# Layer 0 of a graph network: a dense product with a scattered matrix of edge weights, in place of edge-by-edge sums

## The reference, cut to what matters

```python
x = _layernorm(x + _L0_gnn_ref(x, src, dst, edge_weight, weight, bias))
...
# layer 0, with edge_row = src and edge_col = dst
gathered = edge_weight[:, None] * x[edge_col]
neigh = jax.ops.segment_sum(gathered, edge_row, num_segments=N_NODES)
out = x @ w_self + neigh @ w_neigh + bias
```

## Time and profile before

| | us |
|---|---|
| median of 3 runs | 4293.28 |
| lowest and highest run | 4287.72, 4300.4 |
| span of the profiled execution | 5597.1 |
| edge loop of layer 0 in the profile (first to last L606) | 63.5 to 909 |
| rows of layer 1 out in the profile | 1505 |
| look-up of layer 1 in the profile | 1510 to 2010 |

### The profile page before, as it was taken

The page is one execution under the profiler, slowest core; times in us unless marked ns, Lnnn a source line. Parts: engine busy times, 40 slices in busy tenths (PEclk is TensorE's granted clock), DMA queues, the critical chain, the costliest instruction groups (busy, mean ns, idle before and its releaser), DMA issues. The chain is left out here.

```text
span 5597.1 us, 67496 instructions
## 1 busy us (share of the span) xinstructions
PE 3296.1 (59%) x16088; PEld 2121.1 (38%) x16089; DVE 2608.5 (47%) x6268; ACT 1784.1 (32%) x3811; POOL 2329.1 (42%) x2110
## 2 busy tenths in 40 slices
PE   5566663111459965446702655671745565999998
PEld 4444442100337742223701522340623333444454
DVE  7666772010249884447201744680654458021213
ACT  3444441000349953334200133460033346020212
POOL 5777887777230046662174065306046640000000
PEclk7887886555679977667755866895866676999999
DMA  8988885100245532232512500004622231313131
GB/s 223 182 181 177 151 138 127 51 22 0 78 121 149 148 97 86 84 88 91 184 33 63 145 22 21 12 14 131 189 61 86 86 112 60 104 61 104 60 106 40
DMA packets 413937, 543.83 MB, mean 97 GB/s; under 512 B 139432, under 2 KB 303361, under 8 KB 413363
## 3 DMA queue, kind: packets, MB, share of 16 engines
q1 hardware_dynamic: 250806, 305.92, 19.5%
q0 software_dynamic: 126368, 178.93, 15.5%
q10 hardware_dynamic: 36573, 56.91, 2.9%
HBM read 404.03 MB, written 141.04 MB: 97 GB/s over the span
## 5 line engine op out<-in xcount | busy, mean ns | idle before, releaser
L981 PE MATMUL ps<-shared_sb,onehot 128*128 128x264 f32 (+1 forms) x1600 | 597.6, 491 | 381.2 <-issue 238.1
L2053 DVE TENSOR_TENSOR accum<-accum,ps 128x264 f32 (+1 forms) x1248 | 530.8, 425 | 528.1 <-issue 341.8
L606 POOL DMA_INDIRECT t_neigh<-resid_sb,idx_b x416 | 655.9, 1577 | 217.8 <-issue 99.5
L1289 ACT ACTIVATE onehot<-iota,drel 128x128 f32<-128x128 f32 x1248 | 381.7, 388 | 1057.2 <-PE ps L904 697.3
L1040 PE MATMUL ps<-score_sb,shared_sb 128*128 128x512 f16 (+1 forms) x3150 | 641.7, 364 | 17.8 <-DVE shared_sb L2082 17.7
L651 POOL DMA_INDIRECT score_sb<-table,idx_a x192 | 200.1, 1042 | 920.4 <-issue 459.6
L981 PEld LDWEIGHTS ps<-shared_sb,onehot 128*128 128x128 f32 x1600 | 315.2, 229 | 664.5 <-issue 596.7
L771 PE MATMUL ps<-score_sb,onehot 128*128 x832 | 299.8, 523 | 330.7 <-DVE onehot L1737 323.0
L651 POOL DMA_INDIRECT shared_sb<-table,idx_a x384 | 363.0, 945 | 240.1 <-ACT idx_a L1272 129.5
L628 POOL DMA_INDIRECT t_adj<-counts,early_sb x391 | 410.0, 1049 | 122.0 <-issue 122.0
L638 POOL TENSOR_SCALAR onehot<-iota,carry_d 98x512 bf16<-98x512 f32 x28 | 43.6, 1562 | 976.8 <-PE ps L1057 814.0
(11 more groups left out here) (390 smaller groups left out, 6578.7 us busy)
## 6 DMA issues: line engine op xcount, KB each, us to landing
score_sb<-t_adj SPq DMA_DIRECT2D x105, 640.0 KB, 3.9
accum<-t_hot SPq DMA_DIRECT2D x208, 256.0 KB
accum<-t_drel SPq DMA_DIRECT2D x208, 128.0 KB
shared_sb<-t_key SPq DMA_DIRECT2D x104, 256.0 KB
t_hot<-shared_sb SPq DMA_DIRECT2D x104, 256.0 KB
t_adj<-accum ACTq DMA_DIRECT2D x70, 320.0 KB
shared_sb<-t_adj SPq DMA_DIRECT2D x35, 640.0 KB, 9.3
t_neigh<-accum ACTq DMA_DIRECT2D x4, 3328.0 KB
```

Of the source, the lines that this page charges most:

```text
L606: pool.indirect_dma_start(t_neigh[u], bass.IndirectOffsetOnAxis(ap=idx_b[:, q * L0H + u:q * L0H + u + 1], axis=0), msg[:, q * L0H + u, :], ...
L981: pe.matmul(ps[:, RING[(HU * h + u) % len(RING)], 0:w], onehot[:, h % 2 * HU + u, :], around[g][place(g, i, h)][:, u, 0:w], start=True, st ...
L1289: last = act.activation(onehot[:, h % 2 * HU + u, :], iota[:, 0:P], ACT.Abs, bias=drel[:, bass.ds(step + u, 1)], scale=-1.0)
L2053: dve.tensor_tensor(to, to, bank.unsqueeze(1), ALU.add).then_inc(step_acc, 1)
```

## The change

The neighbour sums become one dense product. For each edge, DVE sums the weights of all edges of its tile that have the same key; POOL writes the 391 x 128 sums to their cells of a DRAM matrix `t_w` of 26 x 128 rows by 3200 columns, in 4 bytes (42.6 MB, zeroed at the start by ACT). Rows are destinations, with the 98 rows of the last tile taking cells that a tile's run shares with the tile before. The product x^T times this matrix gives the neighbour sums already turned, and the turns and table sums go. The matrix is loaded in two parts of columns (2048 and 1152), 26 tiles each, three buffers per part. Each tile of the first part waits until all scatters have landed. Between the tiles of the second part PE makes 16 of the 25 products with the layer's weights. The edge loop shrinks to 98 quads of compares. Other moves: the copy of `t_lo` and the weights of layer 1 are issued right after SP's loop, the bias fold of layer 1 is done ahead.

```diff
@@ constants
-L0U, L0H = 16, 4
-L0N = L0U // L0H
-L0IT = S // L0U
-L0K = S // L0H
+L0H = 4
+QUADS = ET // L0H
+FIRST = 12
+WT = NT + 1
+WCOLS = [2048, NP - 2048]
+W_ZERO = 1280
@@ buffers
+        w_ring = [resid_sb[:, 0:3 * WCOLS[0]].rearrange("p (r n) -> p r n", r=3),
+                  score_sb[:, NT * GW:NT * GW + 3 * WCOLS[1]].rearrange("p (r n) -> p r n", r=3)]
+        w_banks = [[(4 * f + v, 0, v * 512, 512) for f in range(DC) for v in range(4)],
+                   [at for f in range(DC) for at in ((2 * f, 0, 0, 512), (2 * f + 1, 0, 512, 512), (4, f * P, 1024, P))]]
@@ order of the scatters, and the order of products
+        for quads in [range(8 * m, 8 * m + 8) for m in range(10)] + [range(80, 89), range(89, QUADS)]:
+            w_order += [L0H * q + b for b in range(L0H) for q in quads if L0H * q + b < EDGES_T]
+        product_order = [("l0", t) for t in range(20)] + [("l1", t) for t in range(GRP)] + [("l0", t) for t in range(20, NT)]
+        product_order += [("l1", t) for t in range(GRP, NT)]
+        UNDER = 16
@@ SP
-            with sp.Fori(0, L0IT) as i:
...
+            with sp.Fori(0, QUADS // 2) as i:
+                for h in range(2):
+                    sp.wait_ge(*count("counted", 2 * i + h + 1))
+                    sp.wait_ge(*count("key_used", 2 * i + h + 1))
+                    sp.sem_inc(done("sp_go"), 1)
+                    sp.dma_start(wide_key[:, h, :], on_each(t_key, i * 2 * L0H + h * L0H, L0H)).then_inc(key_in[h], 16)
+                    sp.dma_start(wide_w[:, h, :], on_each(a["ew2"], i * 2 * L0H + h * L0H, L0H)).then_inc(key_in[h], 16)
...
+            w_rows = t_w.rearrange("(r c) o -> r (c o)", c=NP)
+            for part in range(2):
+                first = 0 if part == 0 else WCOLS[0]
+                for t in range(WT):
+                    if part == 0 and t < NT:
+                        sp.wait_ge(*count("w_landed", QUADS))
+                    elif part == 0:
+                        sp.wait_ge(*count("w_landed", QUADS))
+                    if t >= 3:
+                        sp.wait_ge(*count("w_used", part * NT + t - 2))
+                    rows_t = P if t < NT else EQ
+                    put(w_ring[part][0:rows_t, t % 3, :], w_rows[t * P:t * P + rows_t, first:first + WCOLS[part]], w_in[3 * part + t % 3])
@@ POOL
-            def l0_scatter(k, q, first=False):
...
+            def weight_sums():
+
+                pool.wait_ge(*count("w_zero", 16 * (WT // 2)))
+                for n, j in enumerate(w_order):
+                    pool.wait_ge(*count("counted", j // L0H + 3))
+                    if n >= 2 * NACC:
+                        pool.wait_ge(*written(0, n - 2 * NACC))
+                    pool.indirect_dma_start(t_w, bass.IndirectOffsetOnAxis(ap=w_x[:, j:j + 1], axis=0), w_sum[:, j:j + 1],
+                                            None).then_inc((moved + gath)[n % (2 * NACC)], 16)
...
+            weight_sums()
@@ PE
+            def weighted_rows(part, between=lambda t: None):
+
+                for t in range(WT):
+                    pe.wait_ge(w_in[3 * part + t % 3], 16 * (t // 3 + 1))
...
+                    for n, (bank, col, first, w) in enumerate(w_banks[part]):
...
+                        lhs = hrows[:, t, f * P:(f + 1) * P] if t < NT else x_carry[:, f * P:(f + 1) * P]
+                        mm = pe.matmul(ps[:, bank, col:col + w], lhs, w_ring[part][0:rows_t, t % 3, first:first + w], start=(t == 0 and col == 0), stop=(t == NT and (part, n) != (1, 2)))
...
+                    between(t)
...
+            weighted_rows(0)
...
+                def layer0(t):
+                    own = slice(t * P, (t + 1) * P)
+                    product("l0", t, [(cols[:, c, own], weights[:, c, 0:D]) for c in range(DC)]
+                            + [(neigh_w[:, c, own], weights[:, DC + c, 0:D]) for c in range(DC)])
...
+                weighted_rows(1, under)
+                for t in range(UNDER, 20):
+                    layer0(t)
+                layer1(0)
+                for t in range(20, NT):
+                    layer0(t)
+                for g in range(1, NG):
+                    layer1(g)
@@ ACT
+            no_sums = flat_a[:, 5376:5376 + W_ZERO].unsqueeze(1).to_broadcast([P, 2 * NP // W_ZERO, W_ZERO])
+            for part in t_w.rearrange("(k p n w) o -> k p n (w o)", k=WT // 2, p=P, w=W_ZERO):
+                act.dma_start(part, no_sums).then_inc(done("w_zero"), 16)
@@ DVE, one quad of the loop
+            def compare(i, h):
+                k = 2 * i + h
+                dve.wait_ge(key_in[h], 32 * i + 32)
                 dve.wait_ge(*count("counted", k + 2))
+                for u in range(L0H):
+                    at = bass.ds(k * L0H + u, 1)
+                    dve.scalar_tensor_tensor(w_eq[:, u, :], wide_key[:, h, :], adj_f[:, at], wide_w[:, h, :], ALU.is_equal, ALU.mult, accum_out=w_sum[:, at])
                 for u in range(2):
                     at = bass.ds(k * L0H + u, 1)
                     last = dve.tensor_scalar(key_eq[:, u, :], wide_key[:, h, :], adj_f[:, at], 0.0, ALU.is_equal, ALU.add, accum_out=counted_f[:, at])
                 last.then_inc(done("counted"), 1)
```

More of the change, by code:

```diff
@@ L349, in written @@
+        quads_by = []
+        for n in range(len(w_order)):
+            issued = set(w_order[:n + 1])
+            q = quads_by[-1] if n else 0
+            while q < QUADS and all(j in issued or j >= EDGES_T for j in range(L0H * q, L0H * q + L0H)):
+                q += 1
+            quads_by.append(q)
+        quads_by.append(0)
+        def written(n, j):
             u = j % (2 * NACC)
-            return (moved + gath)[u], 16 * (L0K if u < NACC else 0) + 16 * (j // (2 * NACC) + 1)
+            return (moved + gath)[u], 16 * (n * scattered[u] + j // (2 * NACC) + 1)
@@ new lines, in _ @@
+            put(weights_l1[:, :, 0:D], a["L1_gnn_W"].rearrange("(c p) n -> p c n", p=P), done("ld_w1"))
+            sp.wait_ge(*count("rows_out", 48))
+            by_steps = t_lo.rearrange("n (j r) e -> (n j) r e", j=QU)
+            for i in range(S // UN + 1):
+                sp.dma_start(by_steps[i * UN:(i + 1) * UN], t_lo1[i * UN:(i + 1) * UN, :].unsqueeze(1).to_broadcast([UN, P // QU, P])
+                             ).then_inc(done("lo_out"), 16)
+            sp.wait_ge(*count("need", 1))
@@ new lines, in rooted, with turned_tiles @@
+                def rooted(g):
+                    now = slice(GRP * g, GRP * (g + 1))
+                    act.wait_ge(*count("var_ln0", g + 1))
+                    act.activation(small[:, now, 1], small[:, now, 0], ACT.Sqrt).then_inc(done("std_ln0"), 1)
+                def turned_tiles(g):
+                    for t in range(GRP * g, GRP * g + GRP):
+                        act.wait_ge(*count("node_turn", t + 1))
+                        act.activation(cols[:, :, t * P:(t + 1) * P], ps[:, t % 4, 0:D].rearrange("p (c n) -> p c n", c=DC), ACT.Copy
+                                       ).then_inc(done("node_turn_ev"), 1)
@@ L1607, in _ @@
             link(dve.tensor_copy(te_last[:, :], te_last_i[:, :, 0]))
+            for b in range(EB):
+                last = dve.tensor_scalar(tiles_le[:, b, :], iota[0:EQ, 0:NT], te_last[:, b:b + 1], None, ALU.is_ge)
+            link(last)
             for b in range(EB):
@@ L2131, in first_layer_nodes @@
                 link(dve.tensor_tensor(resid[:, :, :], hrows[:, :, 0:D], all_rows(row("L0_gnn_bias")), ALU.add))
[L2132 to L2143 removed]
+                for g in range(3):
+                    summed(g)
+                    if g > 0:
+                        centred(0, g, group(g - 1))
@@ L2145, in _ @@
+                for n in (3, 4, 2, 5):
+                    evicted(n, 1)
+                summed(3)
+                centred(0, 3, group(2))
+                summed(4)
+                for g in (3, 4):
+                    centred(0, g + 1, group(g))
             first_layer_nodes()
```

486 lines of the change are left out of this document (180 added, 306 removed).

## The result

| | us |
|---|---|
| changed kernel, median of 8 runs | 4305.92 (4303.21 to 4308.58) |
| kernel before, median of 8 runs beside it | 4294.49 (4287.72 to 4300.4) |
| ratio, 95% interval | 1.0027, 1.0016 to 1.0037 |
| forecast, range | 4336, 4210 to 4435 |

The change costs 11.4 us, a quarter of the 43 us of the sum, and less than the 0.3% that was set as the bound of "the same". This time the profiled execution spans what the runs show, 4301.4 us.

A forecast was written before the change was run, and what follows sets the result against it. POOL's row scatters were taken to bound the edge loop, ending at 909. Layer 1's rows out at 679 + 6 + 313 + 59 = 1057 against 1014 gave +43 us, 4336; range -83 to +142 (4210 to 4435).

The forecast's parts named there:

- everything behind is the same: After layer 1's rows: adjacency ends at 1211, hidden by the 505 us look-up, so nothing behind changes.
- Zeroing: Start of the changed kernel: ACT zeroes 42.6 MB before any scatter, 103 us plus other queue traffic, landed at 145.
- Compares: Edge loop, changed kernel: DVE 4.3 us per quad, 5.15 with loads; 98 quads plus 45 of prologue, about 560.
- Scatters: POOL's 391 scatters of sums at 1.36 us each, 532 us from 145, covering the compares, landed at 679.
- The wait: Before the matrix loads: all scatters must land, so ordering by quads buys nothing; first tile 6 us.
- DVE sets it: Node stage of the kernel before: DVE sets its length, 105 us, putting layer 1's rows out at 1014.
- the last group through ACT and PE 10: End of the node stage before: the last group passes ACT and PE in 10 us, part of the 105.
- A: Zeros landed at 112, scatters 1.26 us each: rows out at 985, -29 us; chance 0.28 with all going this way.
- B: PE's 1.40 us per instruction, seen in the profile, also in timed runs: -4 us; chance 0.16 with near misses.
- Against: the 1304 us: Profile span exceeded the runs' median by 1303.8 us; PE's slow stretches, explaining some 850, were taken as absent from timed runs.
- C: Edge loop before: 0.30 us gaps before POOL's DMAs only under the profiler, loop ends at 719: +143 us, chance 0.2.
- the unexplained 450 us: Some 450 of the profile's 1304 us excess over timed runs, left after PE's slow stretches explained some 850.

The follow-up runs named there:

- paced form: The changed kernel with 3 of the 13 zeroing parts ahead of the loop and ten issued by ACT inside it: 4266.87 us, ratio 0.9941.
- tile_wait: The changed kernel, each of the first 25 matrix loads waiting only for the edge quads that hold its destinations: 4238.5 us, ratio 0.9868.
- tiles_in_loop: The changed kernel with the wait per tile and 21 of 26 first-part tile loads issued inside SP's loop of quads: 4161.59 us, ratio 0.9692.
- before_thin_adj: The kernel before, each of the 391 adjacency scatters writing 16 of its 128 cells: 4253.78 us, ratio 0.9913.
- thin scatters: The kernel before and the changed kernel, each adjacency scatter writing 16 of its 128 cells: 4253.78 and 4295.74 us, ratios 0.9913 and 1.0006.
- before_again: The kernel before, unedited, profiled once more: 4296.74 us, span 4294.9.

## Why the prediction was wrong

The forecast of +43 us missed by 32. The path of the changed kernel came out right almost to the microsecond, partly by luck: zeros that landed early and a first tile, product and tail that were short made up for slow scatters. What it was set against was wrong in two steps: the path of the kernel before, and "everything behind is the same".

| step | forecast | measured |
|---|---|---|
| 1 zeros landed | 145 | 128.9 |
| 2 compares end | 560 | 601.2 |
| 3 scatters, each | 1.36 | 1.43 |
| 3 scatters landed | 679 | 690.5 |
| 4 first tile | 6 | 5.4 |
| 5 dense product | 313 | 309 |
| 6 tail | 59 | 54 |
| rows of layer 1, changed | 1057 | 1058.7 |
| rows of layer 1, before | 1014 | 1031.6 |
| look-up, changed less before | 0 | -19.8 |

**Zeroing.** It had landed by 128.9, 16 us earlier; but its worse effect was not seen: the loads of quads start 57 us later than in paced form, behind stores of keys that go out behind 42.6 MB. The Trainium skill (DMA: Bandwidth & Descriptors, Specifications) gives an HBM limit of about 358 GB/s per core, by which the zeros alone would take 119 us, an estimate. The trace speaks against that limit here: the zeros and the traffic beside them moved 398 GB/s in the first 100 us. So did the row of reads the earlier trace rows.

**Compares.** The pace was right (490 / 98 = 5.0 us a quad against 5.15). The start was 66 us off, at 110.6 and not at 45, since the forecast had the zeros cost the loop 10 us and not delay its first load; the end was 41 us late.

**Scatters.** (688.1 - 128.9) / 390 = 1.43 us. The mean duration, 415.7 / 391 = 1.063, is near the 1.049 of the earlier trace rows; what the sum lacked is POOL's wait for the compares, 26.3 us in 7 waits. The sum had POOL cover the compares. Being 16 us early and 0.07 x 391 = 27 us slow gives the 11.5 us by which the scatters landed late.

**The wait.** That the order by quads buys nothing with this wait is right. Undoing the wait alone is worth 67 us (tile_wait), and 144 with the loads of tiles inside SP's loop (tiles_in_loop).

**The baseline, first failed step.** "DVE sets it", 105 us for the node stage of before. It took 112.5 (919.1 to 1031.6) and, in before_thin_adj, 115.1. DVE did not set it. Its last add starts at 1004.4, 85 us into the stage, where the sum had 95; but "the last group through ACT and PE 10" took 27 us, because at 1004.8 ACT still had the two groups before it to copy out. The first copy of each of the last three groups, in ACT's order of time:

```profile
1006.42 0.40 ACT L1413 ACTIVATE score_sb<-ps 128x272 f32<-128x272 f32 x1 [0.34 <-PE ps L802]
...
1017.03 0.40 ACT L1413 ACTIVATE score_sb<-ps 128x272 f32<-128x272 f32 x1 [1.28 <-PE ps L802]
...
1027.48 0.40 ACT L1413 ACTIVATE score_sb<-ps 128x272 f32<-128x272 f32 x1 [1.07 <-PE ps L802]
```

The five copies of a group take 4.1 us; then come the normalisation and the turns of the next group, for which ACT and PE wait on each other. From one group to the next it is 10.5 us, where the sum had only one such turn. And the loop ended 10 us later than in the one profile that was read. Its last scatter starts between 902.7 and 914.3 in three profiles, so this part is the spread of the kernel before.

**"Everything behind is the same", second failed step,** and the larger one. Hidden work was priced at nothing for the stage that hides it. The adjacency's last scatter came 228 us earlier, and the look-up got 19.8 us shorter; with thin scatters that difference is gone. In sum: 43 - 10 - 7.5 + 1.7 = 27 at the rows, less 20, leaves 7; the two profiles differ by 6.5, the medians by 11.4. The 5 us between these two are not explained; they are within the spread of the runs.

**The rivals.** A (cheap scatters): 1.26 us was reached only at the end of the loop, and the start at 128.9 lay midway between its 112 and the sum's 145; it did not decide. B (the hold is real): held to be unlikely by "Against: the 1304 us". That argument does not hold: the hold can be in the timed runs. The kernel before takes 5640 to 5650 us in timed runs on three chips, and on a fourth that had been free of it. The timed runs of the result were free of it, as the sum assumed; with it the change costs 74 us, where B's sum had -4. C (gaps of 0.30 us only under the profiler): before_again's span, 4294.9, is its time less 2 us, with the gaps in it (304 of them, 96.2 us in all, are POOL's in the loop); the timed runs under the hold are as long as the profile of before and longer, so the unexplained 450 us came with that condition as well, though no run shows in which stretches. The range held the result, and 4305.92 lies in "within 0.3%", which had a chance of 0.16.

## What to carry to other kernels

When the parts that a change removes and adds nearly cancel, the error of the baseline is the error of the forecast: work out the old path's last stage engine by engine, as carefully as the new one. Moving a stream of small DMAs in time changes the price of whatever runs beside it (here 0.075 us per us), even where the stream itself stays hidden. And a profile whose span is not the time of the runs may show another condition of the machine, one that can come back in timed runs, as here, and not the profiler's doing.

## What was not expected of the hardware

- Under a condition that came and went, also on one and the same chip, PE gets on average one instruction per 1.13 to 1.40 us while POOL issues indirect DMAs without a break, in straight code and in the look-up's loop (1.19 us), and the kernel before takes 5640 to 5650 us instead of 4294. With POOL idle PE takes its usual 592 ns for a matmul. DVE and ACT are slower too: in 150 to 600 us of the changed kernel's loop, without any work of PE, DVE does 860 instructions instead of 1109. What sets the condition stays open.
- An indirect DMA of 16 cells of 4 bytes takes POOL 0.849 us, one of 128 cells 0.960; 16 rows of 1 KB with an add 1.27, 128 rows 1.54. Most of it does not depend on the count.
- Zero writes in 5 KB packets, with what ran beside them, moved 398 GB/s in the first 100 us.
- The stores of ACT's 0/1 tiles, 256 KB each, are so delayed beside scatters of 128 cells of 2 bytes that ACT's wait for them is 69.3 us instead of the 37.9 beside scatters of 16 cells, although a full scatter moves only 256 bytes.
